# Attention with a chunked scan: the two largest score levels copied as whole blocks by ScalarE

## The chip, the core and the metric

The kernel runs on one core of one Trainium2 chip. Times are device microseconds of one execution, from launch to end; the profile's span is a little shorter, from the first to the last instruction. Engines: PE is TensorE, ACT ScalarE, DVE VectorE, POOL GpSimd, SP the queue that loads and stores.

## The reference

Attention here is a linear recurrence per head over 2048 tokens with a decay per feature, behind a layer norm; a second layer norm, a mixture of 12 experts (two per token) and a last layer norm follow. Cut to what matters:

```python
xn = layernorm(x) * gamma + beta                # x: 1 x 2048 x 512, 8 heads of 64
w = sigmoid(xn @ Wx @ Ww + bw); k = xn @ Wk; v = xn @ Wv; r = sigmoid(xn @ Wr)
for t in range(2048):                           # per head, state is 64 x 64
    state = (1 - w[t])[:, None] * state + k[t][:, None] * v[t][None, :]
    y[t] = r[t] @ state
x = layernorm(x + y @ Wo)
top_w, top_i = top_k(softmax(x @ gate_w.T), 2)  # 12 experts, weights normalised
x = layernorm(x + sum_e cw[:, e] * ((silu(x @ w1[e].T) * (x @ w3[e].T)) @ w2[e].T))
```

## The kernel before

The recurrence is cut into 16 chunks of 128 tokens. Within a chunk, the influence of token s on a later token t is a score, r[t] times k[s] with the decays between them. The scores are made at seven levels: at the level of block length m, keys in the first half of a block of 2m tokens meet receptances in its second half, each multiplied by the decays up to the middle (`grown` and `kept` copies in the buffer `RL`). TensorE makes all levels into PSUM (`pS`, line 401), and what belongs to each level is put into one 128x128 block per head, `ST`, which is then the right-hand side of the value matmuls (`apply_values`, line 426). The smallest levels need a mask. The level of 32 consists of two whole blocks of 32 x 32 per head, the level of 64 of one whole block of 64 x 64.

Each chunk runs its heads in two halves, two groups of two heads in each. Per half, `mask` (line 1075) on VectorE copies seven levels with a mask (line 1088) and the largest level with a plain copy (line 1091); its semaphore `s_dve` lets TensorE run the value matmuls and then overwrite `pS` with the scores of the next half. From the third masked copy on, each waits until the one before it has ended, since they write the same block.

Every engine's order is written out by hand. TensorE in a chunk: scores of half 0; state read (line 412) and keys turned (line 436); fill-in work; the output projection of the chunk before (lines 463 to 465); value matmuls of half 0; scores of half 1; fill-in work (the projections of later chunks, lines 367 to 369 and 340 to 342) with the state's update (line 446) in it; value matmuls of half 1; a last piece of fill-in work. Odd chunks from 1 to 11 (`FIRST`) begin a new pair of chunks: ScalarE normalises x, TensorE turns it, ScalarE makes its upper half `xh` (line 811) and VectorE its lower half `xl` (line 1073). Even chunks from 2 to 12 (`SECOND`) have one projection more ahead of the value matmuls of half 0. Chunks 13 to 15 run the router's units (`GATE_SLOTS`): TensorE makes a unit into `pA`, and ScalarE has to fetch it before the one after the next.

In the same chunk VectorE, ScalarE and GpSimd prepare the next chunk's levels: receptances by VectorE (lines 732 to 741) and ScalarE (line 687), keys by GpSimd (line 757) and ScalarE (line 700), each level waiting for the one below on both its engines. ScalarE also copies `kbT` (line 916), scales the state (`sdec`, line 931), makes the upper half of y (line 965), and casts the experts' weights in pieces (line 708), whose rest GpSimd subtracts (line 763). Behind the masked copies of half 1 VectorE updates the state (line 1143), in even chunks then makes the decay products of the next pair (line 723), and at the start of the next chunk the lower half of y (`low_y`, line 1207), which TensorE's state read waits for. `PIECES[n]` says how many weight pieces are cast and split in the chunk ahead of n; `split(t)` in ScalarE's chunk is piece t.

Of the kernel before, what the change touches and what calls it, by code (L numbers as in the profile page):

```python
# [20 lines left out]
P = 128  # L21
# [3 lines left out]
S = 64  # L25
PAIR = 2 * P
NPAIR = T // PAIR
NT = T // P
# [3 lines left out]
NL = len(LEVELS)  # L32
NMASK = 7
JOBS = 10
# [18 lines left out]
PIECE_AT = {4: (0,), 5: (1,), 6: (2, 3)}  # L53
PIECES = [2, 4] + [4 if n % 2 == 0 else 3 for n in range(2, NT - 2)] + [0, 0]

# [80 lines left out]
def attention(nc, X, idt, kc, gw, x, wxT, ww, wk, wv, wr, wo, by_feature, ident, masks, consts, gate_w, w_experts, w_split, logitT, early, pA,  # L136
# [10 lines left out]
    with ExitStack() as ctx:  # L147
# [6 lines left out]
        def sem(name):  # L154
            return ctx.enter_context(nc.semaphore(name))
# [74 lines left out]
        s_full = sem("s_full")  # L230
        s_dve = sem("s_dve")
        st_piece = sem("st_piece")
# [102 lines left out]
        def _(pe):  # L335
# [38 lines left out]
            def scores(n, k, half):  # L374


                pair, c = in_pair(k)
                pe.wait_ge(s_dve, n * 2 + (half + 1))
                b = k % 2
# [36 lines left out]
            def apply_values(n, k, half):  # L416

                pair, c = in_pair(k)
                if half == 0 and n // 2 < NPAIR - 1:
                    pe.wait_ge(a_out, done(n // 2, 8 + c))  # L420
                if half == 0 and n // 2 == NPAIR - 1:
                    pe.wait_ge(gate_out, taken("value", c))
                pe.wait_ge(s_dve, n * 2 + (half + 2))
                for g in HALVES_OF[half]:
                    for h in range(2):
                        i = pe.matmul(pY[h * S:(h + 1) * S, 0, g * P:(g + 1) * P],
                                      val[pair][:, c, g * P + h * S:g * P + (h + 1) * S], ST[half][:, 2 * (g % 2) + h, :],
                                      start=False, stop=True, skip_group_check=True)
                i.then_inc(st_used, 1)
# [346 lines left out]
        def _(a):  # L776
# [31 lines left out]
            def high_x(q, par):  # L808

                a.wait_ge(a_out, order(q, 1) + 1)  # L810
                a.copy(xh[par][:, :, :], xf[:, :, :]).then_inc(x_hi, 1)
# [29 lines left out]
            def gate_take(u):  # L841
# [15 lines left out]
                ins.then_inc(gate_out, 1)  # L857

            def chunk(n, k, own, nxt=None, jobs=None):

# [16 lines left out]
                def fill(s):  # L877
                    for d, m in slots[s]:
                        take(q + d, m, (q + d) % 2, n)

                def gating(s):
                    if n in GATE_SLOTS:
                        for u in GATE_SLOTS[n][s]:
                            gate_take(u)
# [32 lines left out]
                if slots is FIRST:  # L917
                    take(q, 0, par)
                    take(q, 1, par)
                    high_x(q, par)  # L920
                if n == NT - 3:
# [5 lines left out]
                if n < NT - 1:  # L927
# [4 lines left out]
                    i.then_inc(sd_ready, 1)  # L932
                gating(1)
                key_levels(4)
                if slots is not FIRST:
                    fill(0)
                gating(2)
                late_norms(2)
# [20 lines left out]
                split(1)  # L959
                fill(1)  # L960
                split(2)
                gating(5)
                fill(2)
# [7 lines left out]
            a.sem_inc(st_used, 2)  # L971
            a.sem_inc(y_out, 1)

            def high(i):
# [69 lines left out]
        def _(v):  # L1044
# [30 lines left out]
            def mask(n, k, half):  # L1075
# [4 lines left out]
                for lv in range(NMASK):  # L1080
                    m = 1 if lv < 2 else 1 << (lv - 1)
                    if lv >= 2:
# [6 lines left out]
                                      pS[:, :, lv * S:(lv + 1) * S].rearrange(shape, m=m)).then_inc(st_piece, 1)  # L1089
                v.wait_ge(st_piece, n * (2 * NMASK) + (half + 1) * NMASK)  # L1090
                v.tensor_copy(ST[half][0:S, :, S:P], pS[0:S, :, NMASK * S:]).then_inc(s_dve, 1)

# [130 lines left out]
            v.wait_ge(setup_done, 1)  # L1223
            v.sem_inc(s_dve, 1)
            v.sem_inc(state_new, 1)
# [770 lines left out]
```

## Time and profile before

| | |
|---|---|
| three runs | 760.46, 763.71, 766.45 us; median 763.71 |
| the profiled execution | 763.16 us; its span 761.3 us, mean granted clock of TensorE 0.987 |
| TensorE busy | 721.4 us (95%) |
| VectorE busy | 502.6 us (66%); of it masked copies 121.2 us (224 of 570 ns on average) |
| ScalarE busy | 346.0 us (45%) |
| GpSimd busy | 305.4 us (40%) |
| from 57 to 440 us (the chunks) | TensorE 369.0 of 383.0 us, VectorE 307.6, ScalarE 221.6, GpSimd 178.7 |

The busy time of TensorE is nearly the span, so the gaps that are left are small, and they are spread over the chunks. What a gap is waiting for is read from the waits and from the instructions in order of time. VectorE and ScalarE have idle time on average, but their work is chained: an instruction of theirs is late when what it needs is late.

### The profile page before, as it was taken

How to read it: one execution, taken by the hardware profiler on the slowest of the kernel's cores; microseconds unless marked ns; L12 is line 12 of the kernel's file. 1: busy time of each engine (PE TensorE's matmuls, PEld its weight loads, DVE VectorE, ACT ScalarE, POOL GpSimd, SP SyncE). 2: the span in 40 equal slices, each digit the busy share in tenths (PEclk: the TensorE clock that was granted, in tenths of full speed). 3: DMA queues.
4: the chain of work that ended last, by engine and by line, in shares of the span. 5: the costliest groups of instructions: out<-in, count | busy, mean ns of one | idle time of the engine just before them, and what ended most of it. 6: DMA issues, size and time to landing. Idle time of an engine off the chain costs nothing. (4 is left out here: it accounts for less than half of the span.)

```text
span 761.3 us, 17944 instructions
## 1 busy us (share of the span) xinstructions
PE 721.4 (95%) x6231; PEld 521.2 (68%) x6232; DVE 502.6 (66%) x1102; ACT 346.0 (45%) x695; POOL 305.4 (40%) x336
## 2 busy tenths in 40 slices
PE   9999899999999999999899987999999999999994
PEld 4777678787787877777576876666666666666641
DVE  3857969879688796887778884444444444444477
ACT  3865654657546576586564212222222222222264
POOL 0574555554655545547311002343343433344210
PEclk9999999999999999999999999999999999999998
DMA  8824365353653536536210037255555555522855
GB/s 332 310 64 149 121 222 167 112 177 103 221 168 111 183 97 203 196 132 198 76 71 15 29 139 276 71 194 204 182 204 207 193 197 203 193 83 96 337 226 196
DMA packets 40123, 126.77 MB, mean 167 GB/s; under 512 B 4224, under 2 KB 4608, under 8 KB 38144
## 3 DMA queue, kind: packets, MB, share of 16 engines
q1 hardware_dynamic: 31024, 99.49, 37.4%
q0 software_dynamic: 6880, 22.55, 8.7%
q10 hardware_dynamic: 2160, 3.93, 1.4%
q8 instruction: 39, 0.64, 0.4%
q14 instruction: 20, 0.16, 0.1%
HBM read 81.13 MB, written 44.83 MB: 165 GB/s over the span
## 5 line engine op out<-in xcount | busy, mean ns | idle before, releaser
L1088 DVE COPY_PREDICATED ST<-msk,pS 128x256 f32<-128x256 uint8 x224 | 121.2, 570 | 51.4 <-issue 24.4
L763 POOL TENSOR_TENSOR piece_parts<-piece,piece_parts 128x1024 f16<-128x1024 f32 x48 | 103.8, 2162 | 96.2 <-ACT piece_parts L708 96.2
L1574 PE MATMUL pH<-ring,xgh 128*128 x344 | 103.7, 301 | 4.6 <-issue 3.5
L757 POOL TENSOR_TENSOR RL<-RL,AM 128x256 f32<-128x256 f32 x96 | 72.5, 755 | 77.6 <-ACT RL L700 71.9
L1575 PE MATMUL pH<-ring,xgh 128*128 x344 | 103.4, 301 | 0.0
L1576 PE MATMUL pH<-ring,xgl 128*128 x344 | 103.4, 301 | 0.0
L1787 DVE TENSOR_TENSOR hid<-pH,sil 128x320 f32<-128x320 f32 x43 | 21.1, 492 | 119.2 <-ACT sil L1658 82.6
L1886 POOL DMA_INDIRECT y_scratch<-ysb,sidx x43 | 42.8, 996 | 138.9 <-DVE ysb L1803 138.9
L401 PE MATMUL pS<-RL 64*128 64x64 f32 (+2 forms) x1536 | 89.1, 265 | 0.0
L401 PEld LDWEIGHTS pS<-RL 64*128 64x128 f32 (+1 forms) x1536 | 84.4, 178 | 2.2
L1658 ACT ACTIVATE sil<-pH 128x320 f32<-128x320 f32 x43 | 18.8, 437 | 130.6 <-PE pH L1576 130.6
L741 DVE TENSOR_TENSOR RL<-RL,AM 128x256 f32<-128x256 f32 x96 | 70.2, 731 | 10.0 <-ACT RL L687 8.1
L367 PE MATMUL pA<-xh,early 128*128 128x256 f16 x256 | 69.9, 273 | 1.5 <-ACT val L805 1.2
L708 ACT CAST piece_parts<-piece 128x1024 f16<-128x1024 f32 x48 | 50.1, 1043 | 43.6 <-DMA piece<-in_w_experts 43.6
L368 PE MATMUL pA<-xl,early 128*128 128x256 f16 x256 | 69.8, 273 | 0.0
L369 PE MATMUL pA<-xh,early 128*128 128x256 f16 x256 | 69.8, 273 | 0.0
L1873 POOL DMA_INDIRECT xg<-x_scratch,gidx x39 | 39.0, 999 | 31.0 <-POOL gidx L1870 22.0
L1592 PE MATMUL pO<-ring,hTh 128*128 x129 | 49.0, 380 | 1.7 <-DVE hTh L1798 1.4
L1574 PEld LDWEIGHTS pH<-ring,xgh 128*128 128x128 f16 x344 | 33.7, 98 | 23.7 <-issue 10.9
L1654 ACT CAST hTh<-pHT 128x384 f16<-128x384 f32 x43 | 20.6, 478 | 63.6 <-PE pHT L1582 63.6
L1593 PE MATMUL pO<-ring,hTh 128*128 x129 | 48.9, 379 | 0.0
L687 ACT COPY RL<-RL 128x256 f32<-128x256 f32 x80 | 32.6, 407 | 27.3 <-DVE RL L733 14.6
(254 smaller groups left out, 1541.5 us busy)
## 6 DMA issues: line engine op xcount, KB each, us to landing
piece<-in_w_experts SPq DMA_DIRECT2D x48, 512.0 KB, 5.0
w_split_scratch<-piece_parts SPq DMA_DIRECT2D x48, 512.0 KB, 3.9
ring<-w_split_scratch SPq DMA_DIRECT2D x12, 2048.0 KB
yin<-y_scratch SPq DMA_DIRECT2D x16, 512.0 KB, 13.1
out_x<-X SPq DMA_DIRECT2D x8, 512.0 KB, 2.8
x_scratch<-X ACTq DMA_DIRECT2D x15, 256.0 KB, 2.0
X<-in_x SPq DMA_DIRECT2D x2, 1536.0 KB, 17.6
RL<-in_wxT SPq DMA_DIRECT2D x4, 256.0 KB, 5.2
```

The costliest lines, as they stand in the source:

```text
L367: pe.matmul(o, wh[name][:, kt, cols], xh[par][:, kt, :], start=(kt == 0), stop=False)
L368: pe.matmul(o, wh[name][:, kt, cols], xl[par][:, kt, :], start=False, stop=False)
L369: i = pe.matmul(o, wl[name][:, kt, cols], xh[par][:, kt, :], start=False, stop=(kt == KT - 1))
L401: i = pe.matmul(o, k_, r_, start=True, stop=True)
L708: a.copy(piece_parts[buf][:, 0, :], piece[buf][:, :]).then_inc(piece_hi, 1)
L741: v.tensor_tensor(next_grown(k, lv, 1), grown(rec, k, lv, 1), factor(c, lv, 0), ALU.mult).then_inc(r_dec, 1)
L757: g.tensor_tensor(next_kept(k, lv, 0), kept(key, k, lv, 0), by, ALU.mult).then_inc(k_dec, 1)
L763: g.tensor_tensor(piece_parts[buf][:, 1, :], piece[buf][:, :], piece_parts[buf][:, 0, :], ALU.subtract).then_inc(piece_lo, 1)
L1088: v.copy_predicated(out[:, :, :, 0 if lv == 0 else 1, :], msk[:, lv, :, :].rearrange(shape, m=m), pS[:, :, lv * S:(lv + 1) * S].rearrange( ...
L1574: pe.matmul(p[:, 0, 0:F], xgh[par][:, k, :], wh, start=(k == 0), stop=False)
L1575: pe.matmul(p[:, 0, 0:F], xgh[par][:, k, :], wl, start=False, stop=False)
L1576: t = pe.matmul(p[:, 0, 0:F], xgl[par][:, k, :], wh, start=False, stop=(k == KT - 1))
```

## The change

`NMASK` falls from 7 to 6. VectorE's `mask` ends with the sixth masked copy; the plain copy is removed there. A new function on ScalarE, `whole_blocks`, waits for all six masked copies of the half and copies the level of 32 as two blocks (lines of 32 partitions, 4 heads, 32 columns) and the level of 64 as one (64 partitions, 4 heads, 64 columns). Its semaphore, `s_out`, takes the place of `s_dve`. In chunks 0 to 12 the copies of half 0 stand behind `kbT` (in odd chunks behind the two `take` calls, ahead of the cast for `xh`); in chunks 13 to 15 behind the third group of router units, which moves ahead of key level 4. Those of half 1 stand behind `fill(1)` and, in the last three chunks, the sixth group of router units. `PIECES` gives chunk 1 two pieces instead of four, and chunks 5 and 9 four instead of three; since chunk n's pieces are cast in chunk n-1, two casts and subtractions leave chunk 0, and one each comes to chunks 4 and 8.

```diff
--- before.py
+++ after.py
@@ -30,7 +30,7 @@
 F16 = mybir.dt.float16
 LEVELS = [1, 2, 4, 8, 16, 32, 64]
 NL = len(LEVELS)
-NMASK = 7
+NMASK = 6
 JOBS = 10
 
 
@@ -51,7 +51,7 @@
 HALVES_OF = ((0, 1), (2, 3))
 GROUP = 4
 PIECE_AT = {4: (0,), 5: (1,), 6: (2, 3)}
-PIECES = [2, 4] + [4 if n % 2 == 0 else 3 for n in range(2, NT - 2)] + [0, 0]
+PIECES = [2, 2] + [4 if n % 2 == 0 or n in (5, 9) else 3 for n in range(2, NT - 2)] + [0, 0]
 
 
 TOP = NL - 1
@@ -228,7 +228,7 @@
         k_kept = sem("k_kept")
         am_ready = sem("am_ready")
         s_full = sem("s_full")
-        s_dve = sem("s_dve")
+        s_out = sem("s_out")
         st_piece = sem("st_piece")
         waited = sem("waited")
         inter_done = sem("inter_done")
@@ -375,7 +375,7 @@
 
 
                 pair, c = in_pair(k)
-                pe.wait_ge(s_dve, n * 2 + (half + 1))
+                pe.wait_ge(s_out, n * 2 + (half + 1))
                 b = k % 2
                 for lv in (0, 1, 3, 4, 5, 6, NL):
                     for g in HALVES_OF[half]:
@@ -420,7 +420,7 @@
                     pe.wait_ge(a_out, done(n // 2, 8 + c))
                 if half == 0 and n // 2 == NPAIR - 1:
                     pe.wait_ge(gate_out, taken("value", c))
-                pe.wait_ge(s_dve, n * 2 + (half + 2))
+                pe.wait_ge(s_out, n * 2 + (half + 2))
                 for g in HALVES_OF[half]:
                     for h in range(2):
                         i = pe.matmul(pY[h * S:(h + 1) * S, 0, g * P:(g + 1) * P],
@@ -856,6 +856,15 @@
                     ins = a.copy(ro.logit[:, i, :], pA[:, bank, 0:E])
                 ins.then_inc(gate_out, 1)
 
+            def whole_blocks(n, half):
+
+                a.wait_ge(st_piece, (n * 2 + (half + 1)) * NMASK)
+                m = S // 2
+                for b in range(2):
+                    low, high = slice(b * S, b * S + m), slice(b * S + m, (b + 1) * S)
+                    a.copy(ST[half][low, :, high], pS[low, :, NMASK * S + b * m:NMASK * S + (b + 1) * m])
+                a.copy(ST[half][0:S, :, S:P], pS[0:S, :, (NMASK + 1) * S:]).then_inc(s_out, 1)
+
             def chunk(n, k, own, nxt=None, jobs=None):
 
                 q, par, slots = jobs or (None, None, [[]] * 4)
@@ -917,6 +926,9 @@
                 if slots is FIRST:
                     take(q, 0, par)
                     take(q, 1, par)
+                if n not in GATE_SLOTS:
+                    whole_blocks(n, 0)
+                if slots is FIRST:
                     high_x(q, par)
                 if n == NT - 3:
                     a.wait_ge(x_lo, NPAIR)
@@ -931,10 +943,12 @@
                         i = a.activation(sdec[:, g, :], state[:, g, :], ACT.Copy, scale=dec_end[mine][:, c, g:g + 1])
                     i.then_inc(sd_ready, 1)
                 gating(1)
+                if n in GATE_SLOTS:
+                    gating(2)
+                    whole_blocks(n, 0)
                 key_levels(4)
                 if slots is not FIRST:
                     fill(0)
-                gating(2)
                 late_norms(2)
                 rec_levels(2)
                 key_levels(5)
@@ -958,8 +972,9 @@
                 late_norms(4)
                 split(1)
                 fill(1)
+                gating(5)
+                whole_blocks(n, 1)
                 split(2)
-                gating(5)
                 fill(2)
                 a.wait_ge(st_used, n * 2 + 4)
                 a.copy(yTh[:, :, :], pY[:, 0, :].rearrange("p (g t) -> p g t", g=KT)).then_inc(y_out, 1)
@@ -970,6 +985,7 @@
 
             a.sem_inc(st_used, 2)
             a.sem_inc(y_out, 1)
+            a.sem_inc(s_out, 1)
 
             def high(i):
 
@@ -1087,8 +1103,6 @@
                     shape = "p h (b m) -> p h b m"
                     v.copy_predicated(out[:, :, :, 0 if lv == 0 else 1, :], msk[:, lv, :, :].rearrange(shape, m=m),
                                       pS[:, :, lv * S:(lv + 1) * S].rearrange(shape, m=m)).then_inc(st_piece, 1)
-                v.wait_ge(st_piece, n * (2 * NMASK) + (half + 1) * NMASK)
-                v.tensor_copy(ST[half][0:S, :, S:P], pS[0:S, :, NMASK * S:]).then_inc(s_dve, 1)
 
             def chunk(n, k, nxt=None, turned=None):
 
@@ -1221,7 +1235,6 @@
             v.memset(ST[0][:, :, :], 0.0)
             v.memset(ST[1][:, :, :], 0.0).then_inc(setup_done, 1)
             v.wait_ge(setup_done, 1)
-            v.sem_inc(s_dve, 1)
             v.sem_inc(state_new, 1)
             v.sem_inc(y_low, 1)
             v.sem_inc(x1_ready, 1)
```

ScalarE in an even chunk (chunk 2), from the second key level to the first weight piece, before:

```order
L700 COPY RL<-RL 128x128x2
L916 COPY kbT<-pM 128x512
L700 COPY RL<-RL 128x64x4
L700 COPY RL<-RL 128x32x8
L931 ACTIVATE sdec<-state,dec_end 128x128 x4
L700 COPY RL<-RL 128x16x16
L797 ACTIVATE key<-pA 128x2x2x128
L687 COPY RL<-RL 128x64x4
L700 COPY RL<-RL 128x4x2x32
L687 COPY RL<-RL 128x32x8
L708 CAST piece_parts<-piece 128x1024
```

and with the change:

```order
L700 COPY RL<-RL 128x128x2
L925 COPY kbT<-pM 128x512
L865 COPY ST<-pS 32x4x32 x2
L866 COPY ST<-pS 64x4x64
L700 COPY RL<-RL 128x64x4
L700 COPY RL<-RL 128x32x8
L943 ACTIVATE sdec<-state,dec_end 128x128 x4
L700 COPY RL<-RL 128x16x16
L797 ACTIVATE key<-pA 128x2x2x128
L687 COPY RL<-RL 128x64x4
L700 COPY RL<-RL 128x4x2x32
L687 COPY RL<-RL 128x32x8
```

The key levels (L700 to RL) and receptance levels (L687) of the next chunk now stand behind the block copies, which wait for VectorE.

ScalarE at the end of chunk 0 and the start of chunk 1, before (L801 and L797 to RL are projections, L965 the upper half of y, L817 the normalised x):

```order
L797 ACTIVATE RL<-pA 128x2x2x128
L708 CAST piece_parts<-piece 128x1024
L805 COPY val<-pA 128x512
L965 CAST yTh<-pY 128x512
L708 CAST piece_parts<-piece 128x1024
L817 ACTIVATE pair_x<-X,nmr,rstd 128x512 x2
```

and with the change:

```order
L797 ACTIVATE RL<-pA 128x2x2x128
L865 COPY ST<-pS 32x4x32 x2
L866 COPY ST<-pS 64x4x64
L805 COPY val<-pA 128x512
L980 CAST yTh<-pY 128x512
L817 ACTIVATE pair_x<-X,nmr,rstd 128x512 x2
```

Two casts of weight pieces are gone there, and the block copies of half 1 have come in.

## Rows read from the trace of the kernel before

**Rows 1.** TensorE's waits, 60 to 430 us: total, times, longest, all us.

```profile
PE pY L426 <- DVE ST L1091: 4.9, 8, 1.0
```

**Rows 2.** TensorE in order of time, chunk 6: start, duration, both us.

```profile
200.43 2.79 PE L401 MATMUL pS<-RL 64*128 64x128 f32 x48
...
219.75 0.66 PE L426 MATMUL pY<-ST,val 128*64 128x128 f32 x8
```

**Rows 3.** VectorE in order of time, chunk 6, the second row from a narrower window.

```profile
203.36 4.55 DVE L1088 COPY_PREDICATED ST<-msk,pS 128x256 f32<-128x256 uint8 x7 [3.58 <-issue]
...
206.90 1.02 DVE L1088 COPY_PREDICATED ST<-msk,pS 128x256 f32<-128x256 uint8 x2
207.95 0.42 DVE L1091 COPY ST<-pS 64x256 f32<-64x256 f32 x1
...
214.42 4.49 DVE L1088 COPY_PREDICATED ST<-msk,pS 128x256 f32<-128x256 uint8 x7
```

**Rows 4.** ScalarE in order of time, chunk 6.

```profile
205.10 0.58 ACT L916 COPY kbT<-pM 128x512 f32<-128x512 f32 x1
205.65 0.41 ACT L700 COPY RL<-RL 128x256 f32<-128x256 f32 x1
...
206.76 1.27 ACT L931 ACTIVATE sdec<-state,dec_end 128x128 f32<-128x128 f32 x4
...
209.66 1.04 ACT L708 CAST piece_parts<-piece 128x1024 f16<-128x1024 f32 x1
```

**Rows 5.** ScalarE's instructions by shape, 360 to 440 us: busy us, mean ns.

```profile
L848 ACT COPY pair_x<-pA 128x512 f32<-128x512 f32 x15 | 8.5, 581 | 8.5 <-PE pA L478 8.4
...
L931 ACT ACTIVATE sdec<-state,dec_end 128x128 f32<-128x128 f32 x8 | 2.5, 390 | 0.0
...
L854 ACT COPY early<-pA 128x48 f32<-128x48 f32 x3 | 0.6, 198 | 2.3 <-PE pA L486 2.2
```

**Rows 6.** Order of time, chunk 7: TensorE, then VectorE, then ScalarE.

```profile
223.53 2.79 PE L401 MATMUL pS<-RL 64*128 64x128 f32 x48
...
231.57 0.66 PE L426 MATMUL pY<-ST,val 128*64 128x128 f32 x8 [0.21 <-DVE ST L1091]
...
244.06 0.66 PE L426 MATMUL pY<-ST,val 128*64 128x128 f32 x8
...
231.01 0.42 DVE L1091 COPY ST<-pS 64x256 f32<-64x256 f32 x1
231.41 1.23 DVE L1073 TENSOR_TENSOR xl<-pair_x,xh 128x1024 f16<-128x1024 f32 x1
...
238.77 4.51 DVE L1088 COPY_PREDICATED ST<-msk,pS 128x256 f32<-128x256 uint8 x7
...
230.33 1.04 ACT L811 CAST xh<-pair_x 128x1024 f16<-128x1024 f32 x1
...
234.56 1.04 ACT L708 CAST piece_parts<-piece 128x1024 f16<-128x1024 f32 x1
```

**Rows 7.** Order of time, chunks 0 and 1: VectorE, ScalarE, VectorE, TensorE.

```profile
57.22 1.31 DVE L1088 COPY_PREDICATED ST<-msk,pS 128x256 f32<-128x256 uint8 x2 [7.31 <-issue]
...
59.12 0.90 ACT L700 COPY RL<-RL 128x256 f32<-128x256 f32 x2
...
79.18 1.99 DVE L723 TENSOR_TENSOR dec_end<-AM 128x8 f32<-128x8 f32 x1
...
75.59 2.79 PE L401 MATMUL pS<-RL 64*128 64x128 f32 x48
82.10 1.53 PE L412 MATMUL pY<-RL,state 128*128 128x128 f32 x8 [3.73 <-issue]
```

**Rows 8.** Busy time by engine from 82 to 86 us; PEclk is the granted clock.

```profile
82.00:86.00 4.00, 3.90 (x21) 3.86 (x22) 3.56 (x7) 1.96 (x5) 1.42 (x2) 0.59 0.81 243
```

**Rows 9.** Order of time, chunk 13: TensorE's value matmuls, ScalarE's fetch.

```profile
381.69 0.66 PE L426 MATMUL pY<-ST,val 128*64 128x128 f32 x8
...
381.83 0.58 ACT L852 COPY logitT<-pA 128x512 f32<-128x512 f32 x1 [2.84 <-PE pA L481]
```

## The prediction

> **What bounds the kernel now.** I read the page first: by its table of engines TensorE is busy nearly all the time, so the time is its instructions plus the gaps between them, and a change to VectorE and ScalarE counts only where it moves such a gap. The engine's waits over the attention stage come next: the value matmuls wait for the score block eight times, 4.9 us in all and 1.0 us at most [rows 1]. Then the instructions in order of time, to see what ends just before TensorE needs it. All times are microseconds from the span's start, written "s+x" where s is the end of a chunk's first score matmuls.
>
> In even chunk 6 the scores end at 203.22 = s, and the second value matmuls start at 219.75 = s+16.53 [rows 2]. The first masked copies start at s+0.14 and the second ones at 214.42 = s+11.20 [rows 3]; seven of them with the plain copy behind take 5.0, so VectorE is done at s+16.2 and TensorE, 0.14 behind it, has 0.2 in hand: none of VectorE's 5.0 us is free there, yet none is paid. In odd chunk 7 (s = 226.32) the first value matmuls wait 0.21 for the plain copy, and the second ones start at 244.06 = s+17.74 [rows 6], again with little in hand (masked copies from 238.77, plus 5.0).
>
> **What each half gains and pays.** Removed on VectorE: the seventh masked copy and the plain copy. In chunk 6 the last two masked copies take 1.02 from 206.90, 0.43 or 0.44 each with 0.15 between, so the sixth ends at 207.33; the plain copy ends at 208.37, 1.04 later [rows 3]. In chunk 7 TensorE follows the plain copy's end, 231.43, by 0.14 [rows 6]. So today the block is usable 1.18 after the sixth masked copy, and VectorE is free 1.0 later than it will be.
>
> Added on ScalarE: two copies of 32x128 elements and one of 64x256, from PSUM, which no row shows. Bounds: ScalarE's copies of 48 columns from PSUM take 0.20 and those of 512 columns 0.58; a 128-column one with a scale takes 0.39 [rows 5]. Low end, all three at 0.20 and each started 0.1 before the last one ends (four of those 0.39 take 1.27 together in rows 4): 0.40 us for the three. High end, 0.39, 0.39 and 0.58: 1.16. I take the straight line between 48 and 512 columns, 0.26, 0.26 and 0.37, less the two overlaps: **0.71 us**, and 0.61 until ScalarE's next instruction; these are PSUM copies without a scale, as the 48-column row is.
>
> The Trainium skill ("VectorE: DVE Perf Modes", section on the TRN2 errata) speaks against the edit: every small ScalarE instruction pays its fixed cost again, so tiles should be large. Its cycles would make the three copies 0.86 us without overlap, and the time 4 to 5 us longer than my sum. No row here shows this shape.
>
> Handing over from ScalarE to VectorE takes 0.04 (the cast of 230.33 ends at 231.37, VectorE starts at 231.41 [rows 6]); I take that for the other direction too, and 0.12 to TensorE. So the block is usable 0.04+0.71+0.12 = 0.87 after the sixth masked copy instead of 1.18: **a gain of 0.3 us per half**, if ScalarE stands ready. That condition is what the rest is about, since ScalarE runs in order and is now held until the sixth masked copy.
>
> **Even chunks (2 to 12).** The hold stands behind the copy to kbT and ahead of key levels 2 and 3. Today key level 2 starts at 205.65 = s+2.43 [rows 4]. Now ScalarE waits for s+4.11, copies, and starts it at s+4.11+0.04+0.61 = s+4.76. From there to the first weight piece its own work runs 3.7 (4.01 in rows 4; I take off 0.3, an estimate, for GpSimd, which is further ahead by then), so the piece's cast moves from 209.66 = s+6.44 to s+8.46. VectorE's levels 3 to 6 go by ScalarE's receptance levels on both sides of that cast, and one of them always waits behind GpSimd's piece: the second masked copies come 4.76 after the cast in chunk 6 and 4.21 in chunk 7 (234.56 to 238.77) [rows 3, 4, 6]. With ScalarE late the second pattern applies, so they start at s+12.67 instead of s+11.20. Six of them take 3.93, then 0.87: TensorE may go on at s+17.47 where it is ready at s+16.53. **+0.94 per even chunk.** In chunk 10 ScalarE normalises two tiles there and is late already; I count half. 5.5 x 0.94 = +5.2.
>
> **Odd chunks (1 to 11).** The hold stands ahead of the cast that makes xh. In chunk 7 that cast goes from 230.33 = s+4.01 to s+4.76, and VectorE, which is free earlier than now, waits for it to make xl: +0.7, and the whole chain behind it up to the second masked copies, 12.45 today, moves to s+13.2 [rows 6]. Usable at s+13.2+3.93+0.87 = s+18.0; TensorE, which no longer waits its 0.21 for the first block, would be there at s+17.53. Wait +0.45 each, 6 x 0.45 = +2.7. The waits at the first block go: five of the eight in rows 1, 0.5 each, -2.5. Together **+0.2**.
>
> **Chunk 0 and the two pieces.** The hold delays chunk 0's key levels from 59.12 to 57.22+3.96+0.65 = 61.8; 0.6 to 0.8 of these 2.7 is a wait of ScalarE's further on that goes, so chunk 0's second value matmuls, and with them the scores of chunk 1, come about 1.9 later [rows 7]. Against that, chunk 0 hands no third and fourth piece to GpSimd any more. Today VectorE's decay products stand behind these (the last one, 8 columns wide, takes 1.99), then comes the low half of y, and TensorE, whose scores end at 78.38, waits 3.73 until 82.10 [rows 7]. That wait goes: it continues at 78.38+1.9 = 80.3, **-1.8**. After the wait of 3.73 the granted clock was 0.59 for 4 us [rows 8], so for most of them on its half level, 1.2 GHz, which cost about 4 x 0.41 = 1.6. The new wait in chunk 0, 2.7 with the 0.8 that is there now, is likely to bring the same fall, so I count nothing for it; if not, -3.4 in all. The pieces come back in chunks 4 and 8, where GpSimd's extra 2.1 us meets VectorE's decay products just ahead of an odd chunk: nothing if they miss each other, 1 each if not; **+1** in all.
>
> **Chunks 13 to 15.** Here the hold stands behind router steps. In chunk 13 TensorE's gate matmuls end, it starts the value matmuls at once, at 381.69, and ScalarE fetches the gate's result from 381.83, 0.58 long [rows 9]. Now the block copies follow that fetch: 0.14+0.48+0.71+0.12 = +1.45, and the same in its second half behind the value fetch. Chunk 14 has both again, but waits 0.7 in each half today: 2 x 0.65. In chunk 15 VectorE's list work, not TensorE, sets the end, and 1.0 comes off it ahead: -0.8. The early end of chunk 12 on VectorE gives back 0.45 to a wait for the router's first norms. 2.9+1.3-0.8-0.5 = **+2.9**.
>
> The stage of the experts is untouched: its weights are loaded from pieces split long before.
>
> **Sum:** +5.2 +0.2 -1.8 +1 +2.9 = +7.5 on the profiled execution of 763.16 us (its span is 761.3; it is 0.55 below the median shown): **770.7 us**. About 30 of the block-copy triples stand on the path, so each 0.1 us of their price is 3 us.
>
> **Rivals.** (A) The forecast, ScalarE's order costs more than VectorE gains: 0.55, its own range 766 to 776.
> (B) The copies are cheap, and it isn't slower. One mechanism, the price of the three copies, decides: at the low end of 0.40 even chunks pay 0.3 (+1.8), odd ones nothing, so that their old waits stay gained (-2.5), chunk 0 keeps its clock (-3.5), pieces +0.5, the end +1.3: 760.8. It wins below 0.71-7.5/30 = 0.46 us. For it speaks the 48-column row at 0.20; against it that 512 columns cost nearly three times that. 0.2.
> (C) The copies are dear, 1.16: 30 x 0.45 = +13.5, 784. For it speaks the 0.39 for 128 columns with a scale; against it that a scale is what these copies lack. 0.2, most of it for prices between A's and this end. The rule of the Trainium skill named above lies this way, at about 775.
> The remaining 0.05 is for an order of events that I missed, on either side.
>
> **Numbers.** Range 760 to 780: the forecast's own range, B's point and C's nearer part. The shown runs spread by 0.8%, so about 1% is what can be told from no change: below 756.1 only with B and more luck, 0.06; above 771.3 nearly half of A and nearly all of C, 0.46; between, 0.48.
>
> **What would show it.** In the changed profile: the second masked copies of even chunks starting near s+12.7, and of odd ones near s+13.2; a wait of the value matmuls on ScalarE's block copies of about 0.9 in even and 0.45 in odd chunks, none left on VectorE; no wait of 3.7 in chunk 1; the three copies at 0.71 together. It is wrong if ScalarE's key levels 2 and 3 turn out to have slack, so that the second masked copies don't move, or if the copies take under half a microsecond.

## The result, and the profile after

The changed kernel takes 778.1 us (median of 4 runs, 776.85 to 778.21) beside 762.4 for the kernel before on the same chip (4 runs, 760.46 to 766.45): a ratio of 1.0195, 95% interval 1.0149 to 1.0242. It is slower by 1.95%, clear of the noise; 770.7 was forecast. The profiled execution took 778.0 and spans 776.1 us; TensorE is busy for 724.1 us of it (before 721.4), VectorE for 473.6 (before 502.6), ScalarE for 369.7 (before 346.0). VectorE got its 29 us off, and the kernel became 15 longer.

TensorE's waits from 57 to 456 us answer to [rows 1] (what waits, what for, total, times, longest):

```profile
PE pY L426 <- ACT ST L866: 21.0, 21, 3.0
PE pM L463 <- ACT kbT L925: 2.3, 4, 1.2
```

The eight waits on VectorE are now 21 on the last of ScalarE's block copies, and 4.9 us are 21.0. Chunk 6 shows how one arises. Its first scores end at s = 204.78. First the second value matmuls on TensorE, for [rows 2] (columns: start, duration, engine, line, operation, shapes, count, idle before and what ended it):

```profile
222.47 0.66 PE L426 MATMUL pY<-ST,val 128*64 128x128 f32 x8 [1.09 <-ACT ST L866]
```

VectorE in the same chunk, for [rows 3]:

```profile
204.92 3.94 DVE L1104 COPY_PREDICATED ST<-msk,pS 128x256 f32<-128x256 uint8 x6 [2.46 <-issue]
...
212.96 0.43 DVE L741 TENSOR_TENSOR RL<-RL,AM 128x256 f32<-128x256 f32 x1 [0.72 <-ACT RL L687]
213.56 0.43 DVE L741 TENSOR_TENSOR RL<-RL,AM 128x256 f32<-128x256 f32 x1 [0.18 <-ACT RL L687]
214.80 2.85 DVE L741 TENSOR_TENSOR RL<-RL,AM 128x256 f32<-128x256 f32 x2 [0.81 <-ACT RL L687]
217.58 3.91 DVE L1104 COPY_PREDICATED ST<-msk,pS 128x256 f32<-128x256 uint8 x6
```

And ScalarE, for [rows 4]:

```profile
206.34 0.58 ACT L925 COPY kbT<-pM 128x512 f32<-128x512 f32 x1
208.89 0.52 ACT L865 COPY ST<-pS 32x128 f32<-32x128 f32 x2 [1.97 <-DVE ST L1104]
209.43 0.36 ACT L866 COPY ST<-pS 64x256 f32<-64x256 f32 x1
209.69 0.90 ACT L700 COPY RL<-RL 128x256 f32<-128x256 f32 x2
...
212.46 0.39 ACT L687 COPY RL<-RL 128x256 f32<-128x256 f32 x1
...
213.37 1.04 ACT L708 CAST piece_parts<-piece 128x1024 f16<-128x1024 f32 x1
```

Read it from ScalarE upward. It has nothing to do for 1.97 us until the sixth masked copy ends, though its key levels could run. Then its receptance levels (line 687) are late, VectorE waits for them three times (0.72, 0.18, 0.81), the second masked copies start at s+12.80 in place of s+11.20, and TensorE waits 1.09. TensorE could have gone on with the first half's blocks at 208.86+1.08 = 209.94 (1.08 is the time from the sixth masked copy to the value matmuls where a first half waits, as in chunk 7); it needs them at 211.44. ScalarE was held early for something that is used late.

The two forms of the copies, in answer to [rows 5] (count, total, mean in ns):

```profile
L865 ACT COPY ST<-pS 32x128 f32<-32x128 f32 x64 | 16.3, 255 | 46.5 <-DVE ST L1104 45.6
L866 ACT COPY ST<-pS 64x256 f32<-64x256 f32 x32 | 11.7, 365 | 0.4
```

Chunk 7, for [rows 6], with s = 229.04: VectorE, then the second value matmuls.

```profile
235.02 1.23 DVE L1089 TENSOR_TENSOR xl<-pair_x,xh 128x1024 f16<-128x1024 f32 x1 [1.91 <-ACT xh L811]
...
242.38 1.30 DVE L1104 COPY_PREDICATED ST<-msk,pS 128x256 f32<-128x256 uint8 x2
```

```profile
247.28 0.66 PE L426 MATMUL pY<-ST,val 128*64 128x128 f32 x8 [0.54 <-ACT ST L866]
```

Here the chain begins with xl, which waits for the cast behind the block copies; the masked copies start at s+13.34 and the wait is 0.54.

Chunk 0, for [rows 7]: ScalarE's key levels start at 61.78 instead of 59.12, and the second value matmuls wait.

```profile
60.98 0.52 ACT L865 COPY ST<-pS 32x128 f32<-32x128 f32 x2 [1.95 <-DVE ST L1104]
61.51 0.36 ACT L866 COPY ST<-pS 64x256 f32<-64x256 f32 x1
61.78 0.89 ACT L700 COPY RL<-RL 128x256 f32<-128x256 f32 x2
```

```profile
76.46 0.66 PE L426 MATMUL pY<-ST,val 128*64 128x128 f32 x8 [2.97 <-ACT ST L866]
```

Chunk 13, for [rows 9]: ScalarE fetches the gate's result, then copies; below it the value matmuls of chunk 13's first half.

```profile
388.98 0.58 ACT L852 COPY logitT<-pA 128x512 f32<-128x512 f32 x1 [3.08 <-PE pA L481]
...
389.46 0.52 ACT L865 COPY ST<-pS 32x128 f32<-32x128 f32 x2
389.99 0.36 ACT L866 COPY ST<-pS 64x256 f32<-64x256 f32 x1
```

```profile
390.50 0.66 PE L426 MATMUL pY<-ST,val 128*64 128x128 f32 x8 [1.59 <-ACT ST L866]
```

The next three waits of this kind are 1.47, 1.56 and 1.47. Then the clock. Windows of the changed kernel (busy time by engine, then TensorE's granted clock, DMA share, GB/s), around chunk 0's wait and in chunk 14; the first answers to [rows 8]:

```profile
73.00:77.00 4.00, 1.03 (x11) 0.42 (x8) 3.47 (x8) 1.36 (x4) 2.01 (x3) 1.00 0.89 295
77.00:81.00 4.00, 4.00 (x65) 3.82 (x63) 3.35 (x10) 3.08 (x6) 1.00 (x2) 1.00 0.39 119
...
414.00:418.00 4.00, 2.96 (x34) 2.66 (x36) 1.02 (x6) 3.81 (x12) 1.23 (x2) 0.85 0.19 72
418.00:422.00 4.00, 4.00 (x40) 3.76 (x39) 2.42 (x17) 0.27 (x1) 0.00 (x0) 0.50 0.00 0
422.00:426.00 4.00, 4.00 (x30) 1.61 (x29) 3.42 (x7) 0.86 (x2) 0.00 (x0) 0.50 0.00 0
```

In chunk 14 TensorE ran at 0.50, its lower level of 1.2 GHz, for some 10 us (416.8 to 427.1); the kernel before had 1.00 in the whole of that chunk's stretch (404 to 416 us). No clock fell behind the wait of 2.97.

Cut into stages by the start of each chunk's second value matmuls on TensorE (us, each from the profiled execution), where "rest" is the router's end and the experts:

| kernel | chunk 0 at | chunk 1 | chunks 2 to 12 | chunks 13 to 15 | rest | span |
|---|---|---|---|---|---|---|
| before | 74.50 | 26.72 | 263.00 | 73.90 | 323.2 | 761.3 |
| changed | 76.46 | 22.10 | 272.89 | 81.46 | 323.2 | 776.1 |
| changed, second profile | 75.61 | 25.00 | 273.31 | 79.47 | 323.1 | 776.5 |
| pieces_only | 73.46 | 22.06 | 266.54 | 74.05 | 325.8 | 761.9 |
| copies_only | 75.79 | 25.90 | 271.65 | 84.28 | 326.1 | 783.7 |
| tail_on_vector | 75.29 | 26.09 | 273.63 | 73.93 | 326.2 | 775.1 |
| even_later | 76.10 | 26.09 | 268.36 | 79.40 | 325.9 | 775.9 |
| kept_busy | 77.39 | 22.09 | 272.52 | 85.65 | 324.8 | 782.4 |
| hold_moved | 75.92 | 25.00 | 267.70 | 73.88 | 325.3 | 767.8 |
| first_half | 76.07 | 25.08 | 278.38 | 74.46 | 321.7 | 775.7 |
| second_half | 73.34 | 21.63 | 262.91 | 73.66 | 326.4 | 757.9 |
| second_half_16 | 73.22 | 21.63 | 262.69 | 76.00 | 321.9 | 755.4 |
| second_half_old_pieces | 72.88 | 26.37 | 261.31 | 70.98 | 322.4 | 753.9 |
| second_half_late_pieces | 73.32 | 21.63 | 262.84 | 79.28 | 321.0 | 758.1 |

The whole loss lies in chunks 2 to 12 (+9.9) and 13 to 15 (+7.6), less 2.7 ahead of them.

### The profile page after: what moved, and what is told of

It reads as the page before. It is cut to its first block and busy times, and to the rows that moved or that the text cites. A ratio compares the mean times of both kernels' runs of the same rounds, so it can differ in the third digit from the quotient of the medians.

```text
span 776.1 us, 17944 instructions
## 1 busy us (share of the span) xinstructions
PE 724.1 (93%) x6231; PEld 522.1 (67%) x6232; DVE 473.6 (61%) x1038; ACT 369.7 (48%) x791; POOL 300.6 (39%) x336
## 5 line engine op out<-in xcount | busy, mean ns | idle before, releaser
L1104 DVE COPY_PREDICATED ST<-msk,pS 128x256 f32<-128x256 uint8 x192 | 106.9, 590 | 47.8 <-issue 23.4
L757 POOL TENSOR_TENSOR RL<-RL,AM 128x256 f32<-128x256 f32 x96 | 69.7, 726 | 97.4 <-ACT RL L700 91.9
L401 PE MATMUL pS<-RL 64*128 64x64 f32 (+2 forms) x1536 | 91.3, 269 | 0.0
L401 PEld LDWEIGHTS pS<-RL 64*128 64x128 f32 (+1 forms) x1536 | 86.5, 182 | 2.2
L1816 DVE COPY ysb<-pO 128x512 f32<-128x512 f32 x43 | 29.7, 692 | 23.0 <-PE pO L1606 20.7
```

The costliest lines, as they stand in the source:

```text
L401: i = pe.matmul(o, k_, r_, start=True, stop=True)
L757: g.tensor_tensor(next_kept(k, lv, 0), kept(key, k, lv, 0), by, ALU.mult).then_inc(k_dec, 1)
L1104: v.copy_predicated(out[:, :, :, 0 if lv == 0 else 1, :], msk[:, lv, :, :].rearrange(shape, m=m), pS[:, :, lv * S:(lv + 1) * S].rearrange( ...
```

## The experiments

Seven of the kernels (the first four, `kept_busy`, `hold_moved`, `second_half`) mask a number of the expert list in a register for each tile, which adds 1.6 to 3.2 us to "rest"; the expectations call this the bounded list. The other five read the list as 16-bit numbers, and their rest is 321.0 to 323.1. What is compared is therefore the stages of the table; a median "less 2.5" takes the middle of that off.

**The pieces alone** (the kernel before, with the diff's one line of `PIECES`).

> The kernel before with the two weight pieces moved out of chunk 0 and nothing else. Theory (the pieces made the 3.73 us wait in chunk 1, and the hold in chunk 0 hid part of what they give back): the first value matmuls of chunk 1 come 3.73 plus the 1.6 of the clock fall earlier, 88.7 to about 83.4; chunks 5 and 9 give back about 0.5 to 1.2 together; the time is 758 to 760 where the profile of before shows 763.2. Rival (the shorter masked copies on VectorE, not the pieces, made the wait go): the wait of 3.7 stays, 763 or a little over.

763.6 us beside 763.1, ratio 1.0015 (0.9982 to 1.0048), so about 761 less 2.5, where 758 to 760 was expected. Chunk 1 is 4.7 shorter: its wait of 3.73 and the clock fall are gone, as the theory has it. But 3.5 come back in chunks 2 to 12, most of it in chunk 5, which then has the same wait: TensorE's state read waits 2.2 us in two places, 2.0 at most, and the clock falls to 0.57 behind it. Without the six-mask copies, moving the pieces moves the wait.

**The copies alone** (the changed kernel with the old line of `PIECES`).

> The changed kernel with the old places of the weight pieces: six masked copies and ScalarE's block copies alone. Theory (the two parts add up, the copies cost about 18, the pieces give back 3 to 4): 780 to 783, against 778 for the whole change, with the wait ahead of chunk 1's state read there again, and chunk 5's and 9's extra 1 us gone. Rival (the pieces in chunks 5 and 9 are a main part of the loss): 776 or less.

784.9 us, ratio 1.0292 (1.0247 to 1.0336): 782.4 less 2.5, where 780 to 783 was expected. But the wait ahead of chunk 1's state read, which was to come back, did not. The low half of y is made at 80.66, before TensorE has ended its scores:

```profile
79.97 0.69 DVE L1221 TENSOR_TENSOR yTl<-pY,yTh 128x512 f16<-128x512 f32 x1
...
81.26 2.07 PE L412 MATMUL pY<-RL,state 128*128 128x128 f32 x8
```

These scores come late because of the wait in chunk 0 and a half clock from 77.6 to 84.4. Chunk 1's 25.90 is 0.9 above the 25.00 of the kernels with the pieces moved and a half clock of the same length (the second profile of the changed kernel, `hold_moved`). So moving the pieces saves about 0.9 in chunk 1; the rest of the 3.8 to the changed kernel's 22.10 is the clock. In chunks 2 to 12 the move costs 1.2 (272.89 against 271.65). The pieces are not the loss; the higher total goes with more half clock in the tail (405 to 412 and 433 to 443) than in either profile of the changed kernel.

**The tail's copies on VectorE** (chunks 13 to 15).

```diff
-                    gating(2)
-                    whole_blocks(n, 0)
...
+                if n in GATE_SLOTS:
+                    v.wait_ge(st_piece, (n * 2 + (half + 1)) * NMASK)
...
+                    v.tensor_copy(ST[half][0:S, :, S:P], pS[0:S, :, (NMASK + 1) * S:]).then_inc(s_out, 1)
```

> The changed kernel, but in chunks 13 to 15 VectorE makes the three block copies behind its six masked ones, and the router's units on ScalarE stand where they stood before. Theory (ScalarE's order in chunks 13 and 14 makes waits of 1.5 us, and these bring TensorE to half its clock in chunk 14): the waits of 1.5 and the stretch of granted clock 0.5 go together, the last three chunks lose 0 to 1 us against before in place of 7.6: 770 to 772. Rival (the half clock comes from the longer waits of the chunks ahead, or by chance of position): the stretch at half clock stays, 774 to 776. Rival (the three copies are dear wherever they stand): 776 or more.

775.5 us (773.0 less 2.5). The last three chunks take 73.93, as before the change (73.90): all 7.6 are gone, and with them the long half clock. TensorE in chunk 13, both halves, now without a wait:

```profile
392.46 0.66 PE L426 MATMUL pY<-ST,val 128*64 128x128 f32 x8
...
402.12 0.66 PE L426 MATMUL pY<-ST,val 128*64 128x128 f32 x8
```

Where TensorE waits for the three copies on VectorE (chunk 14), it starts 1.1 to 1.2 us behind the sixth masked copy, later than ScalarE's 0.99. So it was not their price by itself that cost the 4.7 us of waits in chunks 13 and 14, it was standing behind the router's fetch. (This run moves the copies to VectorE and the router's units back at once, so the two are not told apart.) The total is 1 us above the 770 to 772 expected, because chunk 1 ran 26.09 in place of 22.10: in this execution the clock did fall behind chunk 0's wait.

**The hold later in even chunks** (2 to 12; from behind `kbT` to behind `fill(0)`).

```diff
+                if n not in GATE_SLOTS and slots is not SECOND:
                     whole_blocks(n, 0)
...
                     fill(0)
+                if slots is SECOND:
+                    whole_blocks(n, 0)
```

> The changed kernel, but in even chunks 2 to 12 ScalarE makes the first half's block copies behind key level 4 and its first fetch of a projection, 1.2 us later, still ahead of TensorE's first value matmuls. Theory (the 1.1 us waits of the second value matmuls come from ScalarE's being held while VectorE makes its masked copies): the second masked copies start about 1 us earlier, near s+11.7, the waits fall from 1.1 to 0.1 to 0.3 in six chunks, 772 to 774. Rival (the waits are the price of the copies and their handover, 0.99 behind the sixth masked copy wherever they stand): waits as they are, 778.

778.8 us (776.3 less 2.5), above the 772 to 774 expected. ScalarE in chunk 6, where s = 205.32, runs its key levels first and copies at the end of the slack:

```profile
209.96 0.59 ACT L797 ACTIVATE key<-pA 128x512 f32<-128x512 f32 x1
210.44 0.51 ACT L865 COPY ST<-pS 32x128 f32<-32x128 f32 x2
210.96 0.37 ACT L866 COPY ST<-pS 64x256 f32<-64x256 f32 x1
211.23 0.40 ACT L687 COPY RL<-RL 128x256 f32<-128x256 f32 x1
```

```profile
216.54 1.30 DVE L1106 COPY_PREDICATED ST<-msk,pS 128x256 f32<-128x256 uint8 x2
```

```profile
221.86 0.66 PE L426 MATMUL pY<-ST,val 128*64 128x128 f32 x8
```

The second masked copies start at s+11.22 (s+11.4 to s+11.8 in chunks 2, 4 and 8), and the wait of the second value matmuls is zero in all six even chunks. Chunks 2 to 12 take 4.5 less. Not six times 1.1: the first halves of chunks 10 and 12 now wait 0.80 for the copies. The total hides the gain: in this profile chunk 1 lost 4.0 and chunk 15 ran at half clock from 425 to 435, and the mean granted clock is 0.979 to 0.981 in all four runs (changed kernel 0.983 to 0.987).

**Both together.**

> Both places of the order put right: even chunks copy the first half later on ScalarE, and chunks 13 to 15 copy on VectorE with the router's units where they were. The wait in chunk 0 stays. Theory (the loss is ScalarE's order, term by term): the even chunks' 4.5 us and the tail's 7.5 us add up: 781 less 12 is 769, and up to 773 if chunk 0's wait brings a stretch at half clock in this run. Rival (what is won in one place is waited for in another, as in chunks 8, 10 and 12 of the kernel with the later hold): 775 or more.

769.5 us, ratio 1.0098 (1.0068 to 1.0127): 767 less 2.5. Chunks 2 to 12 keep 5.2 of the gain and the tail is at 73.88. The two corrections add up, as the theory says. What is left over the kernel before is the odd chunks, the first-half waits of 0.80 in chunks 10 and 12, chunk 0's wait, and a half clock behind it.

**TensorE kept busy in the waits.**

```diff
+                if n in (13, 14):
+                    u = GATE_SLOTS[n][2][-1]
+                    pe.wait_ge(gate_out, u)
+                    busy(pA[:, (u + 1) % 2, :], 11)
                 apply_values(n, k, 0)
...
+                if n == 0:
+                    at = order(0, 9)
+                    pe.wait_ge(a_out, at)
+                    busy(pA[:, (at + 1) % 2, :], 22)
                 apply_values(n, k, 1)
```

> The changed kernel with extra matmuls that nobody reads in TensorE's waits ahead of the value matmuls: 22 in chunk 0's second half (2.97 us of wait), 11 in each half of chunks 13 and 14 (1.47 to 1.59 each). The waits stay as long. Theory (the stretches at half clock follow these waits, and one of them costs about 5 us): no granted clock of 0.5 between chunk 0 and chunk 15 apart from short ones that the kernel before has too; 776 with the 2.7 us that the bounded list costs in the expert stage of these experiments, against 781 with it for the changed kernel. Rival (the half clock does not hang on the waits): a stretch of 8 to 10 us at half clock in chunk 1, 14 or 15 as before, 780 to 781.

782.4 us, ratio 1.0233 (1.0195 to 1.0272): a miss. Windows behind chunk 0's wait and in chunk 15:

```profile
77.00:81.00 4.00, 4.00 (x67) 3.64 (x67) 1.98 (x7) 2.90 (x6) 0.42 (x1) 1.00 0.21 76
...
449.00:453.00 4.00, 4.00 (x26) 3.88 (x24) 2.87 (x5) 0.75 (x2) 0.00 (x0) 0.50 0.00 0
```

With chunk 0's wait filled the clock stays at 1.00 and chunk 1 takes 22.09. But the changed kernel's first profile had that without any filling, so one run doesn't show it. In the tail the filling outlasted the waits (the value matmuls of chunks 13 and 14 start 0.97 to 1.14 us behind the last block copy, where the changed kernel has 0.05 to 0.14) and the half clock came all the same, in chunk 15, as the rival has it. But the profile is one of four runs. Two of the others have a mean granted clock of 0.994 and 0.996 (780.5 and 777.7 us), above all four runs of the changed kernel (0.983 to 0.987); the profiled one has 0.985, the slowest 0.981. So filling these waits does not always keep the clock up; whether it helps in some executions, and why the clock falls in others, is open.

**The changed kernel once more.**

> The changed kernel once more, its expert list read as 16-bit numbers in place of a register operation. Theory: the same waits in every chunk, and the half clock behind the wait of chunk 0, of chunk 13 or 14, or both; time 774 to 780 with the expert stage at its 323 us. Rival (the half clock of chunk 14 belongs to the change and always comes there): again at 416 to 428 and nowhere else.

778.3 us, one run. Windows:

```profile
77.00:81.00 4.00, 4.00 (x46) 3.88 (x44) 2.05 (x7) 2.38 (x5) 1.65 (x2) 0.52 0.19 72
81.00:85.00 4.00, 4.00 (x29) 3.78 (x26) 2.90 (x5) 0.79 (x2) 0.00 (x0) 0.63 0.00 0
...
431.00:435.00 4.00, 4.00 (x32) 3.77 (x32) 4.00 (x18) 0.84 (x2) 0.00 (x0) 0.50 0.17 66
```

The same waits, and the half clock in chunks 1 and 15 where the first profile had it in chunk 14. The two programs differ in the expert list alone, so the place is not fixed by the order of the chunks' work.

**ScalarE for the second half only.** VectorE makes the three block copies of the first half, and those of chunks 13 to 15, itself.

```diff
-                if n not in GATE_SLOTS:
-                    whole_blocks(n, 0)
...
+                if n not in GATE_SLOTS:
+                    whole_blocks(n, 1)
...
+                if n in GATE_SLOTS or half == 0:
+                    v.wait_ge(st_piece, (n * 2 + (half + 1)) * NMASK)
...
+                    v.tensor_copy(ST[half][0:S, :, S:P], pS[0:S, :, (NMASK + 1) * S:]).then_inc(s_out, 1)
```

> ScalarE copies the whole blocks of the second half alone, in chunks 0 to 12; VectorE copies those of the first half and of chunks 13 to 15 itself, behind its six masked copies; the weight pieces stay out of chunk 0. Theory (the first half's hold does the harm, the second half's is free and lets VectorE go on 1.0 us earlier): no wait in chunk 0's second half beyond the old 0.8, odd chunks' first-half waits of 0.5 gone, 757 to 760, with the 2.7 of the bounded list 760 to 763: at or below the kernel before. Rival (the price of the three copies counts in any half): 768 or more.

759.5 us with the masked list, where 760 to 763 was expected; ratio 0.9973 (0.9952 to 0.9995). The same kernel without that load on its experts:

> The kernel in which ScalarE copies the second half's blocks alone, with the expert list read as 16-bit numbers, so that the expert stage is at its 323 us again. Theory: 756 to 757.5, 5 to 6 under the kernel before, the chunks ending at about 432 in place of 438. Rival (the gain of the last run was chance of the clock): 760 or more.

754.8 us (6 runs, 752.3 to 758.3) beside 762.7, ratio 0.990 (0.9867 to 0.9933): faster than both kernels of this case, and 1.2 below the 756 to 757.5 expected. Of the 5.9 us between the profiles' spans 4.6 lie ahead of the router's end, although this profile has a long half clock in chunk 15; 1.3 lie in the rest, where the 16-bit list may have a part. TensorE's waits from 57 to 456 us:

```profile
PE pY L426 <- DVE ST L1109: 4.0, 8, 1.1
...
PE pY L426 <- ACT ST L866: 0.7, 1, 0.7
```

One wait on ScalarE is left of 21. In chunk 7 (s = 220.24) ScalarE starts xh at once and comes to the copies with time to spare; VectorE below it:

```profile
224.26 1.04 ACT L811 CAST xh<-pair_x 128x1024 f16<-128x1024 f32 x1
...
236.63 0.52 ACT L865 COPY ST<-pS 32x128 f32<-32x128 f32 x2 [1.03 <-DVE ST L1101]
237.17 0.36 ACT L866 COPY ST<-pS 64x256 f32<-64x256 f32 x1
```

```profile
224.94 0.42 DVE L1109 COPY ST<-pS 64x256 f32<-64x256 f32 x1
225.33 1.22 DVE L1086 TENSOR_TENSOR xl<-pair_x,xh 128x1024 f16<-128x1024 f32 x1
...
232.69 1.30 DVE L1101 COPY_PREDICATED ST<-msk,pS 128x256 f32<-128x256 uint8 x2
```

The masked copies start at s+12.45, as before the change. ScalarE is held here too, for 1.03 us, but what stands next behind it is a weight piece.

**The same with the pieces in their old places, and in others** (chunks 11 and 13 instead of 5 and 9).

> The same with the weight pieces where the kernel before has them: the block copies of the second half alone. Theory (VectorE's 1.0 us and the pieces are two gains): chunk 1 waits again ahead of the state read, 2.7 to 3.7, chunks 5 and 9 lose their 0.9: about 3 us over the kernel with the pieces moved, 759 to 761. Rival (VectorE's earlier end takes chunk 1's wait with it): 755 to 757.

> The kernel of the first run of this group, with the two extra pieces for chunks 11 and 13 in place of 5 and 9. Theory (the first-half waits of 0.87 in chunks 5 and 9 are the pieces' doing, GpSimd's subtraction meeting VectorE's decay products): these two go to 0.2, a new one of up to 0.9 comes in chunk 11, none in chunk 13 where the pair's decays are no longer made: 0.5 to 1.3 us less. Rival (the waits only move): no difference.

755.8 us, ratio 0.9913 (0.9881 to 0.9945), and 757.1, ratio 0.9927 (0.9899 to 0.9954): three kernels that can't be told apart. With the old places 759 to 761 was expected. Chunk 1 is 4.7 longer, as the theory has it (the state read waits 1.2 and the output projection behind it 2.0, and a half clock of 3.4 follows), but chunks 2 to 12 are 1.4 shorter, and the clock, which fell least in that profile (70.98 in the last three chunks), covers the rest. With the late places the waits of 0.86 and 0.50 in chunks 5 and 9 go to 0.23 and one of 0.87 comes in chunk 11, as expected, but the 0.5 to 1.3 less that was to follow does not show: the waits move, as the rival has it. Where the pieces stand is worth no more than the clock's wandering.

**ScalarE for the first half only.**

> The other half: ScalarE copies the first half's blocks alone, where the changed kernel does, in chunks 0 to 12; VectorE those of the second half and of chunks 13 to 15. Theory (the first half's hold does the harm): the second masked copies start at s+12.8 in even and s+13.3 in odd chunks as in the changed kernel, the value matmuls behind them wait 1.1 to 1.2 and 0.6 to 0.7, chunk 0's second half 3; with the tail's 7.5 gone and no half clock in chunk 15: 769 to 774. Rival (both halves share the loss): 764 to 767.

778.4 us, ratio 1.0218 (1.0161 to 1.0275), as slow as the whole change though its tail is at 74.46. Its waits:

```profile
PE pY L426 <- DVE ST L1109: 15.3, 15, 3.1
PE pY L412 <- issue: 3.3, 3, 1.7
PE pY L426 <- ACT ST L866: 2.3, 4, 0.7
```

In even chunks the second masked copies start at s+12.8 and TensorE waits 1.21 to 1.23 behind them (0.84 in chunk 10), as expected; in odd ones they start at s+13.8 or later, at least half a microsecond later than expected, since the first ones are late as well, and the wait is 0.46 to 0.67. Beyond the 769 to 774 are also 3.3 us of state reads, almost all in chunks 5 and 9: VectorE ends each chunk an extra copy later, and its decay products there meet the pieces' subtraction, as in `pieces_only`. A half clock of 3.4 us follows the first of these waits (183.7 to 187.1), and 278.38 for chunks 2 to 12 is the worst of all. The copies of the first half on ScalarE do the harm, and those of the second half are what lets VectorE go.

## Why the prediction was right, and where it was off

The direction and the reason were right: ScalarE, held in order until the sixth masked copy, cost TensorE more than VectorE's shorter work gave. In the even chunks moving the hold, and nothing else, takes the wait away (`even_later`). In the odd chunks and in chunk 0 the hold was not moved by itself; there the chain in the trace stands for it, and `first_half` and `second_half_16`, in which the waits come and go with the first half's copies on ScalarE. The time, 778.1, lies in the range, but outside the 766 to 776 of the forecast alone, and that is in part luck: the range went above 776 for dearer copies, while the longest single piece of the way there was a half clock in the tail that no term stands for. The profiles differ by 14.8 where the sum had 7.5: 1.2 more in even chunks, 2.2 in odd ones with the pieces, 4.7 in the tail, 0.9 less in chunks 0 and 1. Point by point:

- **The price.** 0.71 was taken for the three copies; they take 0.90 from start to end (208.89 to 209.79). The single ones are as taken, 0.255 and 0.365, but I let them overlap, as the scaled copies do, and they don't: each starts when the one before it has ended. By the Trainium skill's figures ("VectorE: DVE Perf Modes", section on the TRN2 errata) the estimate was 0.86 without overlap; the trace has 0.04 more. ScalarE starts 0.03 behind the sixth masked copy, and TensorE 0.05 behind the last block copy in second halves and 0.14 in first ones, where 0.12 was taken. So the block is usable 0.99 or 1.08 behind the sixth masked copy, not 0.87. In the kernel before it was usable 1.09 in second halves and 1.19 in first ones (1.18 was taken for both). The gain of 0.3 per half was 0.1.
- **Even chunks.** Forecast +5.2; from first to second value matmuls they are 1.06 to 1.19 longer in five and 0.69 in chunk 10, +6.4 in all. The start of the masked copies, s+12.80 for s+12.67, and the price make the difference. Right in mechanism, and shown by the later hold.
- **Odd chunks and the pieces.** Forecast +0.2 and +1. From chunk 3 on the second halves lost 3.0 where 2.25 was forecast, and the first halves, which were to win, lost 0.4: chunks 5 and 9 lost 1.5 where the pieces' subtraction on GpSimd met VectorE, the other three won 1.1. Chunks 2 to 12 together: +9.9 for a forecast of about 6.
- **Chunks 0 and 1.** Forecast -1.8 with a clock fall assumed behind the new wait, -3.4 without. The profile of the result has none, and stands 2.7 ahead at the end of chunk 1. The second profile has the fall, and stands 0.6 ahead. Both cases of the text occur, 0.7 and 1.2 short of the gain forecast. Moving the pieces takes the wait of 3.73 away (`pieces_only`), but the change would have lost most of it without them: with the old pieces it is nothing in `copies_only` and 1.2 in `second_half_old_pieces`.
- **Chunks 13 to 15.** Forecast +2.9, and here the largest error. Chunk 13's two waits came out nearly as worked out (+3.1; 1.59 and 1.47 for 1.45 each), but the 0.45 that was to come back at the router's first norms did not: TensorE waits 2.2 there in both kernels. Chunk 14 was to lose 1.3 and lost 6.1: 0.83 in each half of waits, and 4.4 more while the clock stood at 0.50. I had counted a fall of the clock in chunk 0 and none in the tail, though chunk 13's two waits in a row are what [rows 8] should have made me ask about. Chunk 15 gave back 1.7 where 0.8 was forecast from VectorE's list work; but the kernel before ran at half clock there for 3.4 us (434.3 to 437.7) and the changed one did not, which is 1.7 by itself. With chunk 14's fall taken in, the sum would have been some 775.

Rival C's end, copies at 1.16 and 784, did not come; at 0.90 the price lies between the forecast's and C's, and by the usable 0.99 for 0.87 it explains about 3.6 of the 7.3 us missed (at the prediction's 3 us per 0.1). Nor is the price alone the loss: in `even_later` the same copies leave no second-half wait in the even chunks, and those of the second half in `second_half_16` leave one wait, of 0.7. Rival B's condition, a price below 0.46, did not hold.

What stays open is the half clock. All five profiles in which the tail's copies stand on ScalarE, behind the router's steps, have a stretch of 8 us or more at half clock in chunks 14 or 15; of the nine without, two have one (`second_half_16` from 421 to 435, `second_half_late_pieces`). Six of the seven executions with an unfilled wait of 3 us in chunk 0 have a fall in chunk 1. It goes with waits, then, but not one for one: even the kernel before has three stretches of 3.4 us in the chunks, 10.2 in all, where the changed kernel's first profile has 13.7. In the one profile with these waits filled it came in the tail all the same.

## What to carry to other kernels

An engine with idle time on average is not free at a given place: before handing it a step that waits, look at what stands behind the step in its order, and put the wait where only the consumer of its result is next. Holds of the same price in both halves were a loss of 2%; those of the second half alone, with nothing urgent behind them, a gain of 0.3% with the masked list and 1% with the 16-bit one. And where a forecast adds waits of over a microsecond to a busy TensorE, allow for one stretch at half clock in the range, 3 to 4.5 us here, without hoping to say where it falls.

## What was not expected of the hardware

The place of the half clock changes from one execution of the same chunks to the next (417 to 427 us in one profile of the changed kernel, 77 to 84 and 429 to 439 in the other), while the totals agree within 0.4 us. And ScalarE's copies from PSUM without a scale start 0.27 apart and don't overlap (0.255 long), where the scaled copies of the state start 0.30 apart and take 0.39 each.
